# Two cross attentions in one kernel: probabilities turned in 32x32 blocks by VectorE and moved through DRAM, and ScalarE's squares of keys ahead of VectorE's copies

## The reference, cut to what matters

```
q = norm(x @ Wq)                       # 16 heads of 128
k = norm(context @ Wk)                 # 4 groups of 128 in layer 0, 8 groups in layer 1
v = context @ Wv
scores = q . k / sqrt(128)             # 32 queries x 257 keys for each head and batch
probs  = softmax(scores)
out    = (probs @ v) @ Wo
```

## Time and profile before

| | |
|---|---|
| median of 3 runs | 3686.31 us (3679.96 to 3687.12) |
| the profiled execution | 3681.27 us, span 3679.5 us |
| granted TensorE clock, mean | 0.971 |
| PE busy | 3373.0 us (92%) |
| DVE busy | 2266.2 us (62%) |
| ACT busy | 1870.3 us (51%) |
| DMA engines, dynamic queue | 12.5% |

### The profile page before, as it was taken

One profiled execution on the slowest core, in us unless ns is written; L12 is line 12 of the kernel. 1 busy time (PEld: TensorE's weight loads), 2 busy tenths in 40 slices (PEclk: granted clock), 3 DMA queues, 4 the chain that ended last, 5 costly groups with the idle time before them and its releaser, 6 DMA issues. The chain is left out here.

```text
span 3679.5 us, 75523 instructions
## 1 busy us (share of the span) xinstructions
PE 3373.0 (92%) x25760; PEld 2261.3 (61%) x25760; DVE 2266.2 (62%) x5629; ACT 1870.3 (51%) x5129; POOL 77.7 (2%) x132
## 2 busy tenths in 40 slices
PE   7999999999998989978886899999999999987799
PEld 4666666666662335556674567667667676665555
DVE  4555555555552227668886677777777777767732
ACT  5656556566544653345563554554554555534421
POOL 0000000000000000000000000000000000000000
PEclk9999999999998999999998999999999999998899
DMA  4111111111112020000002111111111111101000
GB/s 137 52 43 51 43 43 51 43 52 50 45 36 75 1 97 34 11 3 6 6 4 87 39 41 44 36 44 44 36 46 44 36 44 43 38 30 49 1 9 14
DMA packets 117807, 147.98 MB, mean 40 GB/s; under 512 B 11968, under 2 KB 95552, under 8 KB 116032
## 3 DMA queue, kind: packets, MB, share of 16 engines
q1 hardware_dynamic: 117696, 146.54, 12.5%
HBM read 138.91 MB, written 7.60 MB: 40 GB/s over the span
## 5 line engine op out<-in xcount | busy, mean ns | idle before, releaser
L436 PE MATMUL x_Kb<-x_cT,x_wk 128*128 128x257 f32 x3072 | 766.8, 384 | 15.7 <-ACT x_sq L698 8.5
L436 PEld LDWEIGHTS x_Kb<-x_cT,x_wk 128*128 128x128 f32 x3072 | 554.5, 191 | 172.7 <-issue 83.7
L473 PE MATMUL x_PC<-x_pT,x_cn 128*128 128x512 f32 x1024 | 475.1, 607 | 4.1 <-DVE x_oT L1012 0.8
L718 ACT ACTIVATE x_pr<-x_pr,x_ntop 128x257 f32<-128x257 f32 x512 | 261.1, 510 | 298.3 <-DVE x_ntop L968 157.6
L698 ACT ACTIVATE x_sq<-x_Kb 128x257 f32<-128x257 f32 x512 | 195.3, 382 | 311.3 <-DVE x_kT L951 305.7
L473 PEld LDWEIGHTS x_PC<-x_pT,x_cn 128*128 128x128 f32 x1024 | 185.0, 191 | 244.0 <-issue 242.0
L951 DVE TENSOR_SCALAR x_kT<-x_Kb,x_vecs 128x257 f32<-128x257 f32 x512 | 245.7, 483 | 75.2 <-PE x_Kb L436 68.8
L455 PE MATMUL x_Sb<-x_kT,x_qT 128*32 128x257 f32 (+1 forms) x4096 | 275.7, 383 | 4.9 <-DVE x_pr L971 3.3
L724 ACT ACTIVATE x_pr<-x_pr,x_rps 128x257 f32<-128x257 f32 x512 | 240.3, 499 | 41.1 <-DVE x_rps L981 40.8
L988 DVE COPY x_pT<-x_PTb 128x512 f32<-128x512 f32 x256 | 176.8, 691 | 119.4 <-PE x_PTb L465 117.4
L1002 DVE SCALAR_TENSOR_TENSOR x_pcT<-x_last,x_cT,x_PC 128x512 f32<-128x512 f32 x256 | 190.3, 745 | 85.4 <-PE x_PC L473 81.2
(11 more groups left out here) (313 smaller groups left out, 5966.1 us busy)
## 6 DMA issues: line engine op xcount, KB each, us to landing
x_cT<-in_ctxT SPq DMA_DIRECT2D x128, 257.0 KB, 2.8
x_cn<-in_ctx SPq DMA_DIRECT2D x128, 256.0 KB, 3.0
x_last<-x_last_row SPq DMA_DIRECT2D x128, 256.0 KB, 3.8
e_w<-in_e_w SPq DMA_DIRECT2D x3, 1152.0 KB, 7.8
c_staged_heads<-in_c_wqk SPq DMA_DIRECT2D x2, 1536.0 KB, 9.7
x_wq<-in_x_wq SPq DMA_DIRECT2D x1, 2048.0 KB, 8.1
x_wo<-in_x_wo SPq DMA_DIRECT2D x1, 2048.0 KB, 13.3
x_last_row<-x_last_rows SPq DMA_DIRECT2D x128, 2.0 KB
```

What stands on the lines that cost most here:

```text
L436: m = pe.matmul(Kb[j % 2][:, 0:SE], wk[:, c, g * HD:(g + 1) * HD], cT[:, b, c, :], start=c == 0, stop=c == HC - 1)
L473: m = pe.matmul(PC[h][:, :], cn[:, b, c, h * P:(h + 1) * P], pT[:, c, :], start=c == 0, stop=c == KC - 1)
L718: act.activation(pr[:, v, :], pr[:, v, :], ACT.Exp, bias=ntop[:, u:u + 1], scale=1.0 if L1 else -1.0, accum_out=ps[:, u:u + 1]).then_inc(e ...
```

## The change

It has two parts.

**Probabilities.** PE's `transpose_probs`, the bank `PTb` and DVE's `copy_probs` are gone. Instead DVE turns the probabilities of each unit in 32x32 blocks (`turn_probs`: one instruction per unit, so four per slot, output `turned`). A block transpose leaves the blocks of the four partition groups where they are, so SP puts them in place by way of DRAM: `store_probs` issues four DMAs of 128 KB in rows of 512 bytes to `probs_row`, and `fetch_probs` waits for all of them and reads 512 KB back to `pT` in rows of 2 KB. In DVE's order `turn_probs` of units 0 and 1 stands in the batch's own slot, ahead of `shift_scores` of unit 2; that of units 2 and 3 in the next slot's key phase. Both write one buffer, so the first waits until the batch before has been moved. `pT` is now ordered by partition group, and the value projection reads it so. `cn` has 2 buffers in place of 4 and is loaded a slot ahead, behind `fetch_probs` on SP.

**Keys in layer 1.** ACT now squares a key as soon as it is projected, and DVE copies it only when the square is done; before, it was the other way round. The positions of the calls in each engine's order are unchanged. PE waits for the copy, which is now the last reader of the bank.

```diff
+        probs_row = nc.dram_tensor(n + "probs_row", [KC * 4, S, 4, UNITS * S], F32, kind="Internal").ap()
-        cn = sb("cn", [P, BT, KC, H])
+        cn = sb("cn", [P, 2, KC, H])
+        turned = sb("turned", [P, KC * 4, UNITS * S])
-        PTb = bank("PTb")
...
+            def load_context_rows(i, b, wait=True):
+                if wait:
+                    sp.wait_ge(pc_done.sem, pc_done.after(i, HC * (b - 1)))
+                sp.dma_start(cn[:, b % 2, :, :], d["ctx"][i * BT + b][0:LAST, :].rearrange("(c p) n -> p c n", p=P)
+                             ).then_inc(cn_in[b % 2].sem, 16)
+            def store_probs(i, b):
+                sp.wait_ge(pt_turned.sem, pt_turned.now(i, 2 * (b + 1)))
+                for a in range(4):
+                    sp.dma_start(probs_row[:, :, a, :].rearrange("m k n -> k m n"), turned[S * a:S * (a + 1), :, :]
+                                 ).then_inc(pt_stored.sem, 16)
+            def fetch_probs(i, b):
+                sp.wait_ge(pt_stored.sem, pt_stored.now(i, b + 1))
+                sp.dma_start(pT[:].rearrange("p c (a n) -> p c a n", a=4),
+                             probs_row.rearrange("(c j) k a n -> (j k) c a n", c=KC)).then_inc(pt_moved.sem, 16)
...
+                    store_probs(i, b)
                     send_last(i, b, nxt)
+                    fetch_probs(i, b)
+                    if (b + 1 < BT or nxt) and not (first and b == 0):
+                        load_context_rows(i + (b + 1) // BT, (b + 1) % BT)
...
-                pe.wait_ge(k_sq.sem, k_sq.after(t, j - 1))
+                last_reader = k_raw if L1 else k_sq
+                pe.wait_ge(last_reader.sem, last_reader.after(t, j - 1))
...
-            def transpose_probs(t, b, p):
-                pe.wait_ge(pn_done.sem, pn_done.now(t, UNITS * b + 2 * p + 2))
-                pe.wait_ge(pt_copied.sem, pt_copied.after(t, 2 * b + p))
-                for v in range(2):
-                    for c in range(KC):
-                        at = v * KC + c
-                        m = pe.transpose(PTb[:, at * P:(at + 1) * P], pr[:, 2 * p + v, c * P:(c + 1) * P], ident[:])
-                m.then_inc(pt_done.sem, 1)
...
-                pe.wait_ge(pt_copied.sem, pt_copied.now(t, 2 * (b + 1)))
+                pe.wait_ge(pt_moved.sem, pt_moved.now(t, b + 1))
+                pe.wait_ge(cn_in[b % 2].sem, cn_in[b % 2].now(t, b // 2 + 1))
...
-                    if g in (LEAD, LEAD + 2):
-                        for t, b in back(i, s, 1, cur, prev):
-                            transpose_probs(t, b, g // 2)
...
-                    act.wait_ge(k_raw.sem, k_raw.now(t, j + 1))
+                    act.wait_ge(k_done.sem, k_done.now(t, j + 1))
                     act.activation(sq[:, g % SQ, :], Kb[j % 2][:, 0:SE], ACT.Square).then_inc(k_sq.sem, 1)
...
             def copy_key(t, b, g):
-                dve.wait_ge(k_done.sem, k_done.now(t, j + 1))
+                dve.wait_ge(k_sq.sem, k_sq.now(t, j + 1))
...
+            def turn_probs(t, b, p):
+                dve.wait_ge(pn_done.sem, pn_done.now(t, UNITS * b + 2 * p + 2))
+                if p == 0:
+                    dve.wait_ge(pt_moved.sem, pt_moved.after(t, b))
+                else:
+                    dve.wait_ge(pc_done.sem, pc_done.after(t, HC * b))
+                for v in (2 * p, 2 * p + 1):
+                    w = dve.transpose(turned[:, :, v * S:(v + 1) * S], pr[:, v, 0:LAST])
+                w.then_inc(pt_turned.sem, 1)
...
-                    if g in (LEAD, LEAD + 2):
+                    if g == LEAD:
                         for t, b in back(i, s, 1, cur, prev):
-                            copy_probs(t, b, g // 2)
-                            if g == LEAD:
-                                turn_last(t, b)
+                            turn_probs(t, b, 1)
+                            turn_last(t, b)
...
                 if cur:
+                    turn_probs(i, s, 0)
                     shift_scores(i, s, 2)
```

More of the change, by code:

```diff
@@ L221, in cross_attention @@
         gate = ctx.semaphore(n + "gate")
-        ctx_in = [sig(f"context_loaded{b}", 1, 16 * 2) for b in range(BT)]
+        ctx_in = [sig(f"context_columns_loaded{b}", 1, 16) for b in range(BT)]
+        cn_in = [sig(f"context_rows_loaded{j}", 2, 16) for j in range(2)]
         ln_sum = sig("ln_stats", 1)
@@ L253, in cross_attention @@
         pn_done = sig("probs_normed", BT * UNITS)
-        pt_done = sig("probs_transposed", BT * 2)
-        pt_copied = sig("pT_copied", BT * 2)
+        pt_turned = sig("probs_turned_in_blocks", BT * 2)
+        pt_stored = sig("probs_stored", BT, 16 * 4)
+        pt_moved = sig("probs_moved", BT, 16)
         last_turned = sig("last_probs_turned", BT)
@@ L321, in _ @@
                          ).then_inc(key_weights, 16)
-            for s in ctx_in:
+            for s in ctx_in + cn_in + [pt_stored, pt_moved]:
                 s.prime(sp)
@@ L377, in _ @@
             load_context(0, 0)
+            load_context_rows(0, 0, False)
             if not L1:
@@ L386, in _ @@
                 load_context(0, b)
+                if b == 1:
+                    load_context_rows(0, 1, False)
             tile(0, True, True)
@@ L397, in _ @@
         def _(pe):
-            for s in (xt_done, q_done, qt_done, k_done, ss_done, s_done, pt_done, pc_done, v_done, y_done):
+            for s in (xt_done, q_done, qt_done, k_done, ss_done, s_done, pc_done, v_done, y_done):
                 s.prime(pe)
@@ L480, in project_values @@
                     for c in range(HC):
-                        w = pcT[:, c, 0, :].rearrange("p (j a q) -> p a j q", j=J, a=4)[:, g]
-                        m = pe.matmul(PC[0][:, g * P:(g + 1) * P].rearrange("p (j q) -> p j q", j=J),
-                                      wv[:, c, g * HD:(g + 1) * HD], w, start=c == 0, stop=c == HC - 1)
+                        m = pe.matmul(PC[0][:, g * P:(g + 1) * P], wv[:, c, g * HD:(g + 1) * HD],
+                                      pcT[:, c, 0, g * P:(g + 1) * P], start=c == 0, stop=c == HC - 1)
                 m.then_inc(v_done.sem, 1)
@@ L842, in _ @@
         def _(dve):
-            for s in (xn_done, xq_done, q_in, q_sum, qn_done, s_read, top_done, r_done, pt_copied, pc_copied,
+            for s in (xn_done, xq_done, q_in, q_sum, qn_done, s_read, top_done, r_done, pt_turned, pc_copied,
                       oq_steps, o_copied, y_read, ln_sum, ln_agg, xq_steps, last_turned):
@@ L957, in shift_scores @@
                 dve.wait_ge(k_rs.sem, k_rs.now(t, b * NG + y + 1))
-                dve.wait_ge(pt_done.sem, pt_done.after(t, 2 * (b - 1) + v // 2 + 1))
+                dve.wait_ge(pt_turned.sem, pt_turned.after(t, 2 * (b - 1) + v // 2 + 1))
                 if v == 0:
@@ L981, in invert_sum @@
                 dve.reciprocal(rps[:, u:u + 1], ps[:, u:u + 1]).then_inc(r_done.sem, 1)
-            def copy_probs(t, b, p):
-                dve.wait_ge(pt_done.sem, pt_done.now(t, 2 * b + p + 1))
+            def turn_probs(t, b, p):
+                dve.wait_ge(pn_done.sem, pn_done.now(t, UNITS * b + 2 * p + 2))
                 if p == 0:
+                    dve.wait_ge(pt_moved.sem, pt_moved.after(t, b))
+                else:
                     dve.wait_ge(pc_done.sem, pc_done.after(t, HC * b))
-                    dve.wait_ge(pc_copied.sem, pc_copied.after(t, HC * b))
-                dve.tensor_copy(pT[:, :, 2 * p * P:2 * (p + 1) * P].rearrange("k c (v r) -> k v c r", v=2),
-                                PTb[:, :].rearrange("k (v c r) -> k v c r", v=2, c=KC)).then_inc(pt_copied.sem, 1)
+                for v in (2 * p, 2 * p + 1):
+                    w = dve.transpose(turned[:, :, v * S:(v + 1) * S], pr[:, v, 0:LAST])
+                w.then_inc(pt_turned.sem, 1)
             def turn_last(t, b):
```

15 lines of the change are left out of this document (7 added, 8 removed).

## The result

The changed kernel takes 3806.26 us (median of 4 runs, 3795.6 to 3808.51) against 3683.14 for the kernel before: a ratio of 1.033, with a 95% interval of 1.0304 to 1.0355. The profiled execution has a span of 3805.0 us and a mean granted clock of 0.962. That lies in the range of 3690 to 3820, but outside the 3715 to 3790 that the forecast gave its own sum: the loss is 123 us where the sum had 63.

The account below looks back on a forecast made before the run. PE was busy 95% or more, but its waits decide: layer 0's -11 and layer 1's +74 make +63 us on 3681.3, so 3744, plus 5 to the median: 3748 us. Range 3690 to 3820; the forecast's own 3715 to 3790.

Parts of the forecast that it names:

- Layer 0, key phase: Without transposes keys wait for ACT's squares; of 1.1 us only 0.53 is left, in slots 1, 2 and 3.
- Layer 0, slot 3: turn_probs waits for ACT's norming, scaling of unit 2 comes 1.33 late, and the next slot 0's values 0.9 later.
- the clock rival: Layer 1: PE busy about 85%, gaps make the clock dip once a tile, +29 us, giving 3777; chance 0.12.
- -11: Layer 0's total in us: -0.7 us per tile, from -0.53 x 3 + 0.9, times 16.
- Layer 1, key phase: PE goes at the bank's pace, so no transpose time returns; DVE's copies come 0.1, 0.25, 0.3 and 0.25 later.
- Layer 1, middle: DVE's copies of keys 5 and 6 wait for squares behind exponentials; slots lose 1.5, 0.8, 1.0 and 0.4 us.
- signs of being wrong: Layer 1's middle not later, PE waiting for probs_moved, or the clock below 1.00 in layer 1.
- so it costs nothing: The move through DRAM takes 7.5 us, with room of 9.3 in layer 0's slot 3 and more elsewhere.
- the move's upper bound of 9.8: Top of the 6.7 to 9.8 us range for store and fetch of the probabilities through DRAM; 7.5 was taken.
- The rival of the other side: PE's removed transposes count: 141 us in full gives 3545, or 3615 with half; chance 0.12.
- the sum of +63: Both layers together: -11 us in layer 0 and +74 us in layer 1.
- a slower move: Rival: store and fetch take 12 us, not 7.5, delaying layer 0 by 92 us, so 3840; chance 0.12.

Follow-up runs that it names:

- norm_first: Changed kernel with layer 0's norm_tokens ahead of turn_probs of units 2 and 3 and turn_last in DVE's slot 0: 3776.79 us, ratio 1.0255.
- best: Changed kernel, old layer 1 key order, layer 0's norm_tokens first and units 0-1 turn_probs late, 199 memsets ending core attention's DVE program: 3676.87 us.
- squares_first_alone: Kernel before with only the new order of layer 1's keys, PE still transposing the probabilities: 3736.44 us, ratio 1.0156.
- squares_ahead: Changed kernel with ACT's squares of keys 5 and 6 each ahead of the exponential they stood behind in layer 1: 3761.29 us, ratio 1.0215.
- 199 memsets: Changed kernel with 199 one-column memsets at the start of layer 0's DVE program, moving where later loops lie in memory: 3776.18 us, ratio 1.0262.

## Why the prediction came out as it did

**Layer 0, key phase: right, but not all of it reached the slot.** Key 3 starts 2.94 after key 0, where 2.95 was forecast (514.10 less 511.15) and 3.49 stood before. But of the 0.53 only 0.14, 0.40 and 0.51 are left in slots 1, 2 and 3 (slots of 20.16, 15.53 and 13.27 us for 20.30, 15.93 and 13.79). The rest is a new gap ahead of `weigh_context` that has no releaser in the profile: 0.45 in slot 1, 0.20 in slot 2, 0.33 in slot 0, none in slot 3 (13.6 us in all), where it was 0.07 or less before. The trace's records of the sequencer, which the timelines leave out, show what lies there. The semaphores of the move and of `cn` had been set 2.6 us earlier or more; but `weigh_context` now waits for both of them, and raises a semaphore behind each, where it waited for one. Before its first weight load in slot 1 the sequencer goes through six instructions in 0.69 us (533.64 to 534.32), and went through three in 0.28 (527.63 to 527.91). No run takes these steps out, so this is read from the trace and not tested.

**Layer 0, slot 3: the step was right, its price was not.** The turn's wait and length came out as said. "The values of slot 0 come 0.9 later" was 1.1 in tiles at full clock and 2.75 in the others. The forecast had the clock as a rival for layer 1 and tested no place of layer 0 for it. It came there, because a wait of 0.55 had grown to 2.2. At full clock a tile would have been as long as before (1.05 saved, 1.08 lost), which turns -11 into about 0, and ten falls of 1.66 make the rest of +16.5; `norm_first` brought back -11.2. The Trainium skill (TensorE: Matmul & The Clock Gate, HAM oscillation) says that waits between bursts of matmuls throttle the engine. Here the trace agrees in part: behind the same 2.22 us the clock fell in ten tiles and stayed up in two.

**Layer 1, key phase: no gain, as said, but no loss either.** Nothing of PE's transposes came back: in `best`, which has the old order of keys and no transposes, layer 1 gains 1.5 us. But the forecast also had DVE's copies later by 0.1, 0.25, 0.3 and 0.25 in the four slots, 0.9 us a tile or 14 us, for the turns. That is the term of the layer that was mis-sized: the turns cost about 2 us with the new order of keys (59.5 less 57.4) and nothing with the old one.

**Layer 1, middle: right in its sum.** The terms of the middle were 1.5, 0.8, 1.0 and 0.4, 3.7 us a tile or 59 in all; `squares_first_alone`, which has nothing else, costs 57.4, with 2.2, 0.7, 0.7 and 0.25 in the slots. That the sum is so close is partly luck, as slot 0 was worse than thought and slots 2 and 3 better. Most of it is queueing behind the exponentials, as `squares_ahead` shows.

**The code's place: not in the sum at all.** 37.8 us. The forecast counted instructions only by their durations. Of its signs of being wrong, the clock below 1.00 in layer 1 came (0.99), and by this: with 199 memsets it is 1.00. PE's lower busy share, by which the clock rival expected it, did not bring it: with 199 memsets PE is busy for 269 of the same 300 us.

**The move: "so it costs nothing" failed twice.** The length was right (7.6 us for 7.5, the first store's issue to the fetch's landing). But the room in layer 0's slot 3, from the first store to `weigh_context`, was 8.1 us (555.06 to 563.17) and not 9.3, so about half a microsecond was left where 1.8 were forecast; with the move's upper bound of 9.8 it would have cost there, so that it cost nothing in the tiles after the first was luck in part. And at each layer's end there is no next slot, which the sum left out: 8.0 and 7.6 us. PE waits for the move there (6.34 and 9.55) and once in tile 1 (0.98), which the forecast had named as a sign of being wrong.

**The rival of the other side** (PE's work counts in full) is ruled out: the most that layer 0 gained in any run was 16.1 us, and layer 1 1.5, of 141, the 16.1 with `norm_tokens` moved as well.

So the sum of +63 was right in sign by its largest term alone, layer 1's middle. Two terms were off, to opposite sides (layer 0 at full clock by 11 us, the turns in layer 1's key phase by 12), and three things it lacked (the clock in layer 0 with 16.6 us, the code with 37.8, the ends with 15.6) made the loss twice as great. That the time still fell within 3690 to 3820 is luck: that range was made wide for the clock case and a slower move, and most of what filled it is the code's place.

## What to carry to other kernels

Moving work off the busiest engine pays only where that engine isn't already waiting there; read the pace of the buffer it fills before counting its instructions. When an instruction is made to wait for another engine, price what stands ahead in *that* engine's queue: most of the new key order's cost was the exponential in front of the square. And after any edit look for waits with no releaser at a loop's first instruction, and for the end of the pipeline, where a hidden latency has nothing to hide behind.
